# Routed experts in a graph and attention layer: one loop per expert, one step at least, and the projection of an expert's last step addressed by a register

## The reference

```python
logits = t @ gate_w.T + gate_b                    # t: 6250 x 512, 8 experts
top_v, top_i = jax.lax.top_k(softmax(logits), 2)  # two experts per node
hr = gelu(einsum('td,efd->etf', t, rw1) + rb1)    # routed experts: 512 -> 256
oe = einsum('etf,edf->etd', hr, rw2) + rb2        # 256 -> 512
out = shared(t) + einsum('etd,te->td', oe, cw)    # two shared experts for all nodes
```

## Time and profile before

| | |
|---|---|
| median of 3 runs | 2250.5 us (2247.77 to 2253.26) |
| the profiled execution | 2250.51 us, its span 2248.9 us |
| mean granted TensorE clock | 0.973 of 2.4 GHz |
| TensorE matmul busy | 2042.3 us, 91% |
| steps of the routed stage | 59 (59 stores to `yd`, L948) |

### The profile page before, as it was taken

One profiled execution on the slowest core, in us unless ns is written; L12 is line 12 of the kernel. 1 busy time (PEld: TensorE's weight loads), 2 busy tenths in 40 slices (PEclk: granted clock), 3 DMA queues, 4 the chain that ended last, 5 costly groups with the idle time before them and its releaser, 6 DMA issues. The chain is left out here.

```text
span 2248.9 us, 46227 instructions
## 1 busy us (share of the span) xinstructions
PE 2042.3 (91%) x12932; PEld 1367.6 (61%) x12933; DVE 1551.8 (69%) x3789; ACT 1082.8 (48%) x2118; POOL 1275.6 (57%) x1370
## 2 busy tenths in 40 slices
PE   4898897899999999999999999983999999789998
PEld 2544454566666666666666666652666666557776
DVE  6888896577877788778877887874444444346666
ACT  3555664555646564656565556522343434223332
POOL 3665665777777777777777777711322222243433
PEclk9999999899999999999999999996999999899999
DMA  8637553788888888888888888852554545567775
GB/s 278 223 113 250 189 184 117 218 272 262 257 263 270 263 261 266 268 262 257 266 261 254 256 268 253 262 199 94 155 164 156 162 155 163 155 195 254 246 263 194
DMA packets 190000, 497.24 MB, mean 221 GB/s; under 512 B 42012, under 2 KB 54812, under 8 KB 188152
## 3 DMA queue, kind: packets, MB, share of 16 engines
q0 software_dynamic: 92720, 309.47, 46.4%
q1 hardware_dynamic: 66505, 135.52, 17.3%
q10 hardware_dynamic: 30719, 51.60, 6.1%
HBM read 373.91 MB, written 122.50 MB: 221 GB/s over the span
## 5 line engine op out<-in xcount | busy, mean ns | idle before, releaser
L665 POOL DMA_INDIRECT region<-table,idx x122 | 116.5, 955 | 356.2 <-PE bank L1312 268.8
L625 POOL DMA_INDIRECT region<-table,ebuf x225 | 225.5, 1002 | 82.6 <-issue 81.7
L625 POOL DMA_INDIRECT Wff<-table,ebuf x225 | 218.4, 971 | 74.0 <-issue 73.4
L334 PE MATMUL bank<-Wff,region 128*125 128x512 f16 (+1 forms) x636 | 245.1, 385 | 13.1 <-DVE region L2061 8.0
L335 PE MATMUL bank<-Wff,region 128*125 128x512 f16 (+1 forms) x636 | 244.1, 384 | 0.0
L336 PE MATMUL bank<-Wff,region 128*125 128x512 f16 (+1 forms) x636 | 244.0, 384 | 0.0
L632 POOL DMA_INDIRECT Wff<-table,ebuf x200 | 196.6, 983 | 61.0 <-issue 60.4
L632 POOL DMA_INDIRECT region<-table,ebuf x200 | 193.8, 969 | 61.0 <-issue 61.0
L1149 PE MATMUL bank<-region,ohs 128*125 128x512 f16 x850 | 192.4, 384 | 10.5 <-DMA region<-table,ebuf 10.4
L1149 PE MATMUL bank<-Wff 128*125 128x512 f16 x850 | 188.3, 380 | 0.0
L2026 DVE COPY region<-bank 128x1024 f16<-128x1024 f16 x60 | 41.5, 692 | 178.4 <-PE bank L1312 178.4
(11 more groups left out here) (327 smaller groups left out, 5504.5 us busy)
## 6 DMA issues: line engine op xcount, KB each, us to landing
yd<-region ACTq DMA_DIRECT2D x59, 512.0 KB, 3.1
x2d<-region SPq DMA_DIRECT2D x25, 512.0 KB
table<-region SPq DMA_DIRECT2D x25, 512.0 KB, 4.6
region<-x2d SPq DMA_DIRECT2D x25, 512.0 KB, 5.1
table<-region POOLq DMA_DIRECT2D x50, 250.0 KB, 3.4
xnt<-region POOLq DMA_DIRECT2D x25, 500.0 KB, 4.0
region<-xnt SPq DMA_DIRECT2D x25, 500.0 KB, 5.4
x2t<-region SPq DMA_DIRECT2D x25, 500.0 KB
```

What stands on the lines that cost most here:

```text
L334: wmm(ps, xh, wh, start=first, stop=False)
L625: pool.indirect_dma_start(out=ring[j][:, s, :], out_offset=None, in_=table, in_offset=bass.IndirectOffsetOnAxis(ap=ebuf[j][:, 2 * s:2 * s ...
L665: pool.indirect_dma_start(out=tg[:, c, :], out_offset=None, in_=table2, in_offset=bass.IndirectOffsetOnAxis(ap=idx[:, 2 * turn + c:2 * tur ...
```

## The change

Experts 1 to 7 get one step at least instead of two (expert 0 keeps two, and only it keeps its step written out by hand). For experts 1 to 7 the step ahead of the loop goes and the loop runs from `lo` to `hi - 1`. Which expert a projection belongs to (e - 1 in the expert's first step, e later) is now computed in registers from the loop's counter, `e - 1 + ((r - lo + 255) >> 8)`, and the second weights on TensorE and the second bias on DVE are addressed with it.

```diff
+        routed_ff = Wff[:, 0:NE].rearrange("p b n -> p (b n)")
+
+        def w2_at(at, part, c):
+            at_c = nc.s_assert_within(at + (half_ff + part * 2 * D + c * D), 0, (NE - 1) * FFB + FFB - D,
+                                       skip_runtime_bounds_check_because="at is the place of one expert's weights")
+            return routed_ff[:, bass.ds(at_c, D)]
+
+        def of_last_step(e, lo, r):
+            past_first = nc.s_assert_within(r - lo, 0, CAP // CH, skip_runtime_bounds_check_because="an expert has tokens / CH steps, rounded up")
+            return e - 1 + ((past_first + 255) >> 8)
...
# ACT
-                step(e, lo)
-                if e:
-                    store_rows(lo)
-                with act.Fori(lo + 1, hi) as r:
+                if e == 0:
+                    step(0, 0)
+                with act.Fori(lo if e else 1, hi) as r:
                     step(e, r)
                     store_rows(r)
...
# TensorE
-                hidden(e, lo)
-                turn_rows(lo + 1)
-                if e:
-                    project(e - 1, lo)
-                with pe.Fori(lo + 1, hi) as r:
+                if e == 0:
+                    hidden(0, 0)
+                    turn_rows(1)
+                with pe.Fori(lo if e else 1, hi) as r:
                     hidden(e, r)
-                    turn_rows(r + 1)
-                    project(e, r)
-            project(NE - 1, hi)
+                    if e == 0:
+                        turn_rows(r + 1)
+                        project(functools.partial(w2, 0), r)
+                    else:
+                        at = pe.snap(of_last_step(e, lo, r) * FFB, min_val=0, max_val=(NE - 1) * FFB)
+                        turn_rows(r + 1)
+                        project(functools.partial(w2_at, at), r)
+            project(functools.partial(w2, NE - 1), hi)
...
# DVE, the count of steps
-            ts(sched2[:, 0:NE], CN[:, 0:NE], -0.5 + 0.5 / CH, 2.0, ALU.add, ALU.max).then_inc(stepped, 1)
+            ts(sched2[:, 0:1], CN[:, 0:1], -0.5 + 0.5 / CH, 2.0, ALU.add, ALU.max).then_inc(stepped, 1)
+            ts(sched2[:, 1:NE], CN[:, 1:NE], -0.5 + 0.5 / CH, 1.0, ALU.add, ALU.max).then_inc(stepped, 1)
...
# DVE, the loop
-                turned_rows(lo + 1)
-                if e:
-                    made(e - 1, lo)
-                low(lo)
-                with dve.Fori(lo + 1, hi) as r:
+                if e == 0:
+                    turned_rows(1)
+                    low(0)
+                with dve.Fori(lo if e else 1, hi) as r:
                     turned_rows(r + 1)
-                    made(e, r)
+                    if e == 0:
+                        made(b2bc[:, 0, :], r)
+                    else:
+                        at = nc.s_assert_within(of_last_step(e, lo, r) * D, 0, (NE - 1) * D,
+                                                skip_runtime_bounds_check_because="the last step's expert is e or the one ahead of it")
+                        made(b2bc.rearrange("p e n -> p (e n)")[:, bass.ds(at, D)], r)
                     low(r)
-            made(NE - 1, hi)
+            made(b2bc[:, NE - 1, :], hi)
```

More of the change, by code:

```diff
@@ L1 @@
+import functools
 from contextlib import ExitStack
@@ L491, in _ @@
             for e in range(NE):
-                lo = sp.value_load(sched2[0:1, e:e + 1], min_val=2 * e, max_val=400) if e else 0
-                hi = sp.value_load(sched2[0:1, e + 1:e + 2], min_val=2 * e + 2, max_val=400)
+                lo = sp.value_load(sched2[0:1, e:e + 1], min_val=e + 1, max_val=400) if e else 0
+                hi = sp.value_load(sched2[0:1, e + 1:e + 2], min_val=e + 2, max_val=400)
                 if e == 0:
@@ L670, in _ @@
             pool.wait_ge(sem["sched2_set"], 1)
-            total = pool.value_load(sched2[0:1, NE:NE + 1], min_val=2 * NE, max_val=400)
+            total = pool.value_load(sched2[0:1, NE:NE + 1], min_val=NE + 1, max_val=400)
             pool.wait_ge(sem["ix_in"], 16)
@@ L951, in _ @@
             for e in range(NE):
-                lo = act.value_load(sched2[0:1, e:e + 1], min_val=2 * e, max_val=400) if e else 0
-                hi = act.value_load(sched2[0:1, e + 1:e + 2], min_val=2 * e + 2, max_val=400)
-                step(e, lo)
-                if e:
-                    store_rows(lo)
-                with act.Fori(lo + 1, hi) as r:
+                lo = act.value_load(sched2[0:1, e:e + 1], min_val=e + 1, max_val=400) if e else 0
+                hi = act.value_load(sched2[0:1, e + 1:e + 2], min_val=e + 2, max_val=400)
+                if e == 0:
+                    step(0, 0)
+                with act.Fori(lo if e else 1, hi) as r:
                     step(e, r)
@@ L1326, in hidden, with project @@
                 last.then_inc(sem["ch_ps"], 1)
-            def project(e, n):
+            def project(weights, n):
                 pe.wait_ge(sem["c_hi"], n)
@@ L1336, in project @@
                         last = three(bank[4 + j][:, :], hTc[:, 0, c, m], hTc[:, 1, c, m],
-                                     w2(e, 0, c), w2(e, 1, c), c == 0, c == 1)
+                                     weights(0, c), weights(1, c), c == 0, c == 1)
                     last.then_inc(sem["cp_ps"], 1)
@@ L1341, in _ @@
             for e in range(NE):
-                lo = pe.value_load(sched2[0:1, e:e + 1], min_val=2 * e, max_val=400) if e else 0
-                hi = pe.value_load(sched2[0:1, e + 1:e + 2], min_val=2 * e + 2, max_val=400)
+                lo = pe.value_load(sched2[0:1, e:e + 1], min_val=e + 1, max_val=400) if e else 0
+                hi = pe.value_load(sched2[0:1, e + 1:e + 2], min_val=e + 2, max_val=400)
                 if e == HELD:
                     pe.wait_ge(sem["ff_back"], 16 * (OVER - 1))
-                hidden(e, lo)
-                turn_rows(lo + 1)
-                if e:
-                    project(e - 1, lo)
-                with pe.Fori(lo + 1, hi) as r:
-                    hidden(e, r)
-                    turn_rows(r + 1)
-                    project(e, r)
-            project(NE - 1, hi)
+                if e == 0:
+                    hidden(0, 0)
+                    turn_rows(1)
+                with pe.Fori(lo if e else 1, hi) as r:
+                    hidden(e, r)
+                    if e == 0:
[6 more added lines that the diff above has]
+            project(functools.partial(w2, NE - 1), hi)
             def hidden_shared(i, b, e):
@@ L1381, in project_shared @@
                         last.then_inc(sem["d_f2"], 1)
-            last_rows = pe.value_load(sched2[0:1, NE:NE + 1], min_val=2 * NE, max_val=400)
+            last_rows = pe.value_load(sched2[0:1, NE:NE + 1], min_val=NE + 1, max_val=400)
             pe.wait_ge(sem["ct_act"], last_rows + 1)
@@ L1985, in _ @@
             dve.wait_ge(stepped, 3)
-            ts(sched2[:, 0:NE], CN[:, 0:NE], -0.5 + 0.5 / CH, 2.0, ALU.add, ALU.max).then_inc(stepped, 1)
+            ts(sched2[:, 0:1], CN[:, 0:1], -0.5 + 0.5 / CH, 2.0, ALU.add, ALU.max).then_inc(stepped, 1)
+            ts(sched2[:, 1:NE], CN[:, 1:NE], -0.5 + 0.5 / CH, 1.0, ALU.add, ALU.max).then_inc(stepped, 1)
             dve.wait_ge(sem["gate_dve"], GATE_STEPS * NG)
             dve.tensor_copy(P0, pos[:].rearrange("p t k -> p (t k)")).then_inc(stepped, 1)
-            dve.wait_ge(stepped, 5)
+            dve.wait_ge(stepped, 6)
             dve.tensor_copy(KA[:, 1:NE + 1], sched2[:, 0:NE]).then_inc(stepped, 1)
@@ L1993, in _ @@
             dve.tensor_copy(P2, P0).then_inc(stepped, 1)
-            n = 8
+            n = 9
             for e in range(1, NE):
@@ L2026, in turned_rows, with made @@
                 dve.tensor_copy(tTc[:, :, :, 128:256], parts16(3, 128)).then_inc(sem["ct_dve"], 1)
-            def made(e, n):
+            def made(bias, n):
                 for j in range(2):
@@ L2032, in made @@
                     dve.wait_ge(sem["y_st"], n * 16)
-                    stt(ysb[:, j, :], bank[4 + j][:, :], sv[:, S_W2:S_W2 + 1], b2bc[:, e, :], ALU.mult, ALU.add).then_inc(sem["y_sb"], 1)
+                    stt(ysb[:, j, :], bank[4 + j][:, :], sv[:, S_W2:S_W2 + 1], bias, ALU.mult, ALU.add).then_inc(sem["y_sb"], 1)
             def low(r):
@@ L2040, in _ @@
             for e in range(NE):
-                lo = dve.value_load(sched2[0:1, e:e + 1], min_val=2 * e, max_val=400) if e else 0
-                hi = dve.value_load(sched2[0:1, e + 1:e + 2], min_val=2 * e + 2, max_val=400)
-                turned_rows(lo + 1)
-                if e:
-                    made(e - 1, lo)
-                low(lo)
-                with dve.Fori(lo + 1, hi) as r:
-                    turned_rows(r + 1)
-                    made(e, r)
+                lo = dve.value_load(sched2[0:1, e:e + 1], min_val=e + 1, max_val=400) if e else 0
+                hi = dve.value_load(sched2[0:1, e + 1:e + 2], min_val=e + 2, max_val=400)
+                if e == 0:
+                    turned_rows(1)
+                    low(0)
+                with dve.Fori(lo if e else 1, hi) as r:
```

(5 more changed lines are left out.)

## The result

The changed kernel takes **2215.58 us** (median of 4 runs, 2215.14 to 2218.49) against 2250.72 us of the kernel before on the same chip (4 runs). The ratio is 0.9847, 95% interval 0.983 to 0.9864: 35 us less. The forecast was 2217.1 us.

A forecast was written before the change was run, and what follows sets the result against it. TensorE and the gather loop were taken as nearly level, the gather slightly later and deciding at short experts. 2250.51 - 29.8 (steps) - 2.7 (stall) - 1 (code) + 0.1 (DVE) = 2217.1 us; range 2210 to 2230.

The forecast's parts named there:

- Part 1, the steps: Routed experts: four wholly empty second steps, of experts 1, 3, 6 and 7, go (59 to 55), worth 29.8 us.
- Part 2, the stall: POOL issues two gathers of expert 6's dropped step 5.87 us apart, not 1.26: gain 2.7 us, bounds 0 and 5.3.
- Part 3, registers on TensorE: TensorE's queue, 53 loop steps: register work for the weights' address is covered by waits and queue, cost 0.
- check of the 0.215 us against the busy time: TensorE, full steps: 0.215 us per 512-column matmul was said to fit 131.53 us of busy time over 21 steps.
- Rival (b): Projection on TensorE: register-addressed matmuls become the bound, slower than before; 2259 us if overlapped, 2396 if not; 5%.
- Part 4, DVE: DVE's register work for the bias's place is hidden; one small instruction ahead of the stage costs 0.1 us.
- Part 5, code: Routed stage: dropping seven written-out steps on TensorE saves one instruction fetch, 1 us, bounds 0 and 3.

The follow-up runs named there:

- experiments 1 and 2: experiment 1, and the kernel before with a minimum of three steps instead of two (64 steps): ratio 1.0147 on a slower chip.
- experiment 1: The changed kernel with the minimum put back to two steps for all experts (59 steps), new loops and register addresses kept: 2246.13 us, ratio 0.9986.
- experiment 3: The changed kernel with empty slots in partition p naming row p of the table instead of all naming row 0: 2207.84 us, ratio 0.9812.
- experiment 4: The changed kernel with TensorE's address written out at each use (ratio 0.9956, slower chip), then instead with 24 more register operations and waits per projection: 2221.68 us.
- experiment 6: The changed kernel with SP's first four shared-stage loads held until the last needed gather landed: 2209.47 us; with the edit of experiment 3 too, 2203.56 us.
- experiment 7: The changed kernel with four more indirect DMAs on POOL into unused space ahead of the routed stage: 2212.85 us, ratio 0.984.

## Why the prediction was right

The time (2217.1 against 2215.6) and its mechanism, steps that go at a gather's price, held. Two terms were too small, by 2.6 and 1.5 us, and the longer first and last intervals, which were not in the sum, took back 2.7. That these misses nearly cancel is luck, and so is part of the closeness.

- **Part 1, the steps** (29.8 us): right. The four intervals measured 7.3 to 7.5 us without the stall, again in experiments 1 and 2, and the stage is 33.7 us longer in experiment 1 than in the changed kernel, which is their sum with the stall (34.4) to within 1 us. The reason given, empty slots that name one row, was confirmed by experiment 3.
- **Part 2, the stall** (2.7, bounds 0 and 5.3): mis-sized, 5.3 was right. The text had it either tied to the step that goes or coming back elsewhere at full price. It is neither. It stands in POOL's 28th trip, and with 55 steps that trip's second list is for rows that no step uses; with 59 and with 64 steps it stands on the chain, in intervals of 12.33 and 10.83 us. That the count of steps fell to where it does no harm is luck of these data. POOL's next work waits for the last store, which lands later, so the stall is covered:

```profile
1944.69 1.17 POOL L705 DMA_DIRECT2D region<-b  x2 [7.63 <-DMA yd<-region]
```

- **Part 3, registers on TensorE** (0): right, with a better reason than the one given. The change adds five instructions of some 50 ns per step, not some fifteen to thirty, and the 12 matmuls of a projection keep their 2.37 us (experiment 4). The idle time of TensorE is 0.36 us a step, not 0.22. The prediction's check of the 0.215 us against the busy time does not come out: 14,336 columns a step at 0.215 us per 512 are 6.02 us, not 6.26; the starts in the trace bear the 0.215 out. Rival (b) needed 0.07 us per matmul uncovered; even 24 more, with waits, cost 0.03 us per matmul on TensorE and 0.10 us per step. The Trainium skill (Advanced Engine Details and Errata, Engine Queue Depths) says 64 for TensorE's queue; the traces agree in so far as the projection's matmuls keep their 0.21 us apart, but no run here shows the number.
- **Part 4, DVE** (0.1): right in cost. What it does is seen: the first L2049 comes 1.67 us behind the copy (1719.48 to 1721.15), where before it came 1.38 us behind, from the copy at 1731.65 to this row of DVE in time in the kernel before:

```profile
1733.03 0.75 DVE L2033 SCALAR_TENSOR_TENSOR region<-bank,sv,region 128x512 f32<-128x512 f32 x1 [0.69 <-PE bank L336]
```

  The 0.29 us are put down to the bias's address, the only thing that the change puts there. The second comes 2.59 us behind the copy in both, so the 0.29 us are gone before anyone waits.
- **Part 5, code** (1, bounds 0 and 3): mis-sized, some 2.5 us, and its cause stays open. The slow second steps of experts 4 and 5 went in the changed kernel and in experiment 1 alike, so they went with the code or its loops and not with the steps. The estimate from the Trainium skill (Advanced Engine Details and Errata, ISA Cache) was three fetches fewer and 3 us; the packets on the instruction queue fell from 24 to 21 in both kernels, and the trace is nearer to its sum than to mine. That a fetch was what made those two gathers slow is not shown, and a fetch alone is not enough. Before, a packet does fall into each of the two slow steps (at 1749.3 to 1749.7 and 1847.7 to 1848.2 us), but another, at 1633.8 to 1634.2, falls into a step of 6.41 us. The changed kernel still has one at expert 4, at 1740.4 to 1740.8, just ahead of a step's second gather (1741.28), and that step takes 6.48 us.
- Not in the sum: the first two and the last interval, 2.7 us longer. The last one holds four loads of 2 MB in all against the gather (experiment 6); why it was 1.6 us longer in the changed kernel than before was not tried. In other kernels with 55 steps and the same loads it took 12.5 (24 more instructions) and 11.2 us (experiment 7), so it may be no more than one execution's scatter.

## What to carry to other kernels

A loop that needs its first trip written out by hand also fixes a least number of trips; look at what the short cases of the real data pay for it, here 4 of 59 steps at 7.3 to 7.5 us. Let padding of an index list point at different rows, and ask whether the last prefetch of a stage fetches anything. When two resources run level, take one away to find the true time of the other: a busy share of 97% hid that the loop was bound by a gather's round trip, and waiting for its two halves one by one took off 19 us more.

## What the runs showed that was not expected

- Two indirect DMAs of 128 rows of 2 KB that (nearly) all name one row make a step of 6.46 us one of 7.3 to 7.5, and with different rows the whole excess goes.
- POOL holds between two gathers in the 28th trip of its loop, whatever the number of steps or of earlier indirect DMAs, with nothing in the profile that it waits for: 5 to 6 us between their starts in most kernels, 3.3 to 9.2 over all.
- TensorE's busy time, added up, says 6.26 us per step; bound by TensorE alone, a step takes 6.10.
- 12 matmuls of 512 columns whose weights are addressed by a register start in 2.37 us, as with fixed addresses. 24 register instructions with satisfied waits, spread between them, make it 2.71 and cost 0.10 us of a 6.46 us step.
